# Attention's small products placed behind the maxima in each step, one product fewer for the turned shift, and maxima and later work one step on

## The reference

```python
b, n, _ = x.shape                      # 2, 1024
h, d = (HEADS, DIM_HEAD)               # 16, 64
qkv = x @ w_qkv.T
q, k, v = jnp.split(qkv, 3, axis=-1)
dots = jnp.einsum('bhid,bhjd->bhij', q, k) * SCALE
m = jax.nn.softmax(dots, axis=-1)
diag = jnp.diagonal(m, axis1=-2, axis2=-1)
mu = diag.mean(axis=-1, keepdims=True)
sd = diag.std(axis=-1, ddof=1, keepdims=True)
keep = jnp.abs((diag - mu) / sd) <= Z_THRESH
valid = keep[..., :, None] & keep[..., None, :]
masked = jnp.where(valid, dots, NEG)
attn = jax.nn.softmax(masked, axis=-1)
attn = jnp.where(row_any, attn, 0.0)
out = jnp.einsum('bhij,bhjd->bhid', attn, v)
return out @ w_out.T + b_out
```

## Time and profile before

| | |
|---|---|
| median of 3 runs | 2136.2 us |
| the profiled execution | 2125.9 us |
| its span, first to last instruction | 2124.6 us |
| PE busy | 1937.1 us, 91% |
| PEld busy | 1311.4 us, 62% |
| DVE busy | 1330.8 us, 63% |
| ACT busy | 1125.2 us, 53% |
| POOL busy | 1174.0 us, 55% |

### The profile page before, as it was taken

The page is one execution under the profiler, slowest core; times in us unless marked ns, Lnnn a source line. Parts: engine busy times, 40 slices in busy tenths (PEclk is TensorE's granted clock), DMA queues, the critical chain, the costliest instruction groups (busy, mean ns, idle before and its releaser), DMA issues. The chain is left out here.

```text
span 2124.6 us, 22033 instructions
## 1 busy us (share of the span) xinstructions
PE 1937.1 (91%) x7432; PEld 1311.4 (62%) x7432; DVE 1330.8 (63%) x2215; ACT 1125.2 (53%) x1586; POOL 1174.0 (55%) x642
## 2 busy tenths in 40 slices
PE   5997899897997984799999999999999999998588
PEld 3772333332775663577777777777777777775366
DVE  5426778887535763566666666666666666665376
ACT  4327566554434444456555555555655556553354
POOL 2440647653443553266666575666665756668454
PEclk9998799899998996899999999999999999999799
DMA  2000000000001003232222222231313131300100
GB/s 88 0 1 1 0 0 1 0 0 0 1 1 44 1 23 71 55 68 49 61 57 53 57 54 65 45 73 37 73 37 73 37 73 37 71 10 12 50 5 16
DMA packets 45921, 74.46 MB, mean 35 GB/s; under 512 B 26800, under 2 KB 28400, under 8 KB 45552
## 3 DMA queue, kind: packets, MB, share of 16 engines
q1 hardware_dynamic: 43744, 72.35, 14.7%
q10 hardware_dynamic: 2032, 0.69, 0.1%
q0 software_dynamic: 32, 0.00, 0.0%
HBM read 20.85 MB, written 1.18 MB: 10 GB/s over the span
## 5 line engine op out<-in xcount | busy, mean ns | idle before, releaser
L1988 POOL TENSOR_TENSOR at_e_lo<-at_e,at_e_hi 128x1024 fp32r<-128x1024 f32 x256 | 613.8, 2398 | 396.7 <-DVE at_e_hi L1961 395.2
L1816 ACT ACTIVATE at_e<-at_ps 128x1024 f32<-128x1024 f32 x256 | 263.0, 1027 | 315.9 <-PE at_ps L1723 315.9
L1808 ACT ACTIVATE at_ps<-at_ps,at_neg_diag 128x1024 f32<-128x1024 f32 x256 | 278.6, 1088 | 116.8 <-DVE at_neg_diag L1876 116.8
L1883 DVE TENSOR_REDUCE at_row_max<-at_ps 128x1 f32<-128x1024 f32 x256 | 311.0, 1215 | 14.9 <-PE at_ps L1702 11.8
L1876 DVE CUSTOM_DVE_ANT_0 at_junk_diag<-at_ps,ident 128x128 bf16<-128x128 f32 x256 | 74.4, 291 | 323.3 <-PE at_ps L1675 323.2
L915 POOL TENSOR_TENSOR mb_work<-mb_work,mb_c 128x1024 f32<-128x1024 f32 x64 | 151.5, 2367 | 169.5 <-DVE mb_work L891 164.7
L1961 DVE CAST at_e_hi<-at_e 128x1024 fp32r<-128x1024 f32 x256 | 220.1, 860 | 30.3 <-ACT at_e L1816 29.8
L386 POOL TENSOR_TENSOR ffn_lo<-ffn_hid,ffn_hi 128x512 fp32r<-128x512 f32 x96 | 124.4, 1298 | 179.3 <-DVE ffn_hi L313 179.3
L1673 PE MATMUL at_ps<-at_k,at_q 128*128 128x512 f32 x512 | 172.6, 419 | 16.2 <-DMA at_k<-at_qk_lo 13.9
L1702 PE MATMUL at_ps<-at_k,at_q 128*128 128x512 f32 x512 | 174.3, 422 | 10.9 <-DMA at_k<-at_mask_rows 8.5
L1742 PE MATMUL at_pv_ps<-at_e_lo,at_v_hi 128*128 128x512 f32 x512 | 161.5, 397 | 8.2 <-POOL at_e_lo L1988 8.1
(11 more groups left out here) (313 smaller groups left out, 3797.9 us busy)
## 6 DMA issues: line engine op xcount, KB each, us to landing
at_q<-at_qk_hi SPq DMA_DIRECT2D x64, 256.0 KB, 3.8
at_k<-at_qk_hi SPq DMA_DIRECT2D x32, 512.0 KB, 5.9
at_q<-at_qk_lo SPq DMA_DIRECT2D x32, 256.0 KB, 6.5
at_k<-at_qk_lo SPq DMA_DIRECT2D x32, 256.0 KB, 6.3
at_recips<-at_recip_row SPq DMA_DIRECT2D x32, 256.0 KB, 3.4
ffn_h_raw<-in_h SPq DMA_DIRECT2D x2, 1024.0 KB, 8.3
at_head_w_raw<-in_w_qkv SPq DMA_DIRECT2D x32, 64.0 KB, 4.2
x<-in_x SPq DMA_DIRECT2D x4, 256.0 KB, 4.9
```

The costliest lines, as they stand in the source:

```text
L1808: act.eng.activation(ps[:], ps[:], ACT.Exp, scale=SCALE, bias=m.small["neg_diag"][s][:, blk:blk + 1], accum_out=m.small["sums"][s][:, blk: ...
L1816: act.eng.activation(m.e[e % 2][:], slot("turned_scores", h, blk)[:], ACT.Exp, scale=SCALE).then_inc(sem["at_exp"])
L1883: dve.eng.tensor_reduce(m.small["row_max"][h % SLOTS][:, blk:blk + 1], slot("best", h, blk)[:], AX.X, ALU.max).then_inc(sem["at_best_out"])
L1988: pool.eng.tensor_tensor(m.e_lo[e % 3][:], m.e[e % 2][:], m.e_hi[e % 3][:].bitcast(F32), ALU.subtract).then_inc(sem["at_lo"])
```

## The change

The order of PE's operations within a step changes: `scores` and `best` come directly behind `turned_scores`, and mean, square, mask and shift behind them. The list of slots and DVE's order follow: DVE now rounds the exponential and takes the maximum ahead of the mean's negation, the keeps, the mask rows and the shift rows. The offsets of `best` and of all that follows it (shift, turned scores, weighing, reciprocals, spread, normalising, output) rise by one, and the loops by one step. By t mod 8: shift and the first part of the values to step 5, the second part to step 1, reciprocals to 2, spread to 3, normalising to 5, output to 7. Scores, statistics, mask and QK keep their steps.

The shift's turn is one transpose of the row maxima instead of two accumulating matmuls; the flags are added on DVE, from the turned rows that `mask_rows` kept. So DVE's `shift_rows` waits for the mask rows and is a sum of two operands, and `mask_rows` waits until the shift rows of two heads before are done.

```diff
-AT_FIRST, AT_LAST = -BLK * 2, BLK * (NH - 1) + BLK * 5
+AT_FIRST, AT_LAST = -BLK * 2, BLK * (NH - 1) + BLK * 5 + 1
...
-AT_SPLIT, AT_QK, AT_SCORES, AT_STATS, AT_MEAN, AT_SQUARE, AT_MASK, AT_BEST, AT_SHIFT = -10, -7, 0, 8, 9, 10, 11, 12, 20
-AT_TURNED, AT_PV, AT_PV_OUT, AT_RECIP, AT_SPREAD, AT_NORM, AT_OUT = 22, 23, 31, 33, 34, 36, 38
+AT_SPLIT, AT_QK, AT_SCORES, AT_STATS, AT_MEAN, AT_SQUARE, AT_MASK, AT_BEST, AT_SHIFT = -10, -7, 0, 8, 9, 10, 11, 13, 21
+AT_TURNED, AT_PV, AT_PV_OUT, AT_RECIP, AT_SPREAD, AT_NORM, AT_OUT = 23, 24, 32, 34, 35, 37, 39
...
     def turn_shift(h):
         pe.wait_ge(sem["at_best_out"], h * BLK + BLK)
         slot_free(pe, c, m, "turn_shift", h)
-        turned = slot("turn_shift", h)[0:BLK, 0:P]
-        pe.eng.matmul(turned, m.small["dropped"][h % SLOTS][:], c.ident[:], start=True, stop=False)
-        pe.eng.matmul(turned, m.small["row_max"][h % SLOTS][:], c.ident[:],
-                      start=False, stop=True).then_inc(sem["at_turn_shift"])
+        pe.eng.transpose(slot("turn_shift", h)[0:BLK, 0:P], m.small["row_max"][h % SLOTS][:],
+                         c.ident[:]).then_inc(sem["at_turn_shift"])
...
         if at := due(t, AT_TURNED, BLK):
             turned_scores(*at)
+        if at := due(t, AT_SCORES, BLK):
+            scores(*at)
+        if at := due(t, AT_BEST, BLK):
+            best(*at)
         if at := due(t, AT_MEAN):
             mean(at[0])
         if at := due(t, AT_SQUARE):
             square(at[0])
         if at := due(t, AT_MASK):
             turn_mask(at[0])
-        if at := due(t, AT_SCORES, BLK):
-            scores(*at)
         if at := due(t, AT_SHIFT):
             turn_shift(at[0])
-        if at := due(t, AT_BEST, BLK):
-            best(*at)
         if at := due(t, AT_QK):
             project(at[0])
...
         if h >= 2:
             dve.wait_ge(sem[f"mask_move{h % 2}"], 16 * (h // 2))
+            dve.wait_ge(sem["at_shift"], h - 2 + 1)
         dve.eng.tensor_copy(m.mask_rows[h % 2][:], slot("turn_mask", h)[0:BLK, 0:P]).then_inc(sem["at_mask"])
...
         dve.wait_ge(sem["at_turn_shift"], h + 1)
+        dve.wait_ge(sem["at_mask"], h + 1)
         if h >= 2:
             dve.wait_ge(sem[f"shift_move{h % 2}"], 16 * (h // 2))
-        dve.eng.tensor_copy(m.shift_rows[h % 2][:], slot("turn_shift", h)[0:BLK, 0:P]).then_inc(sem["at_shift"])
+        dve.eng.tensor_tensor(m.shift_rows[h % 2][:], slot("turn_shift", h)[0:BLK, 0:P], m.mask_rows[h % 2][:].bitcast(F32),
+                              ALU.add).then_inc(sem["at_shift"])
...
         if at := due(t, AT_STATS):
             first_stats(at[0])
+        if at := due(t, AT_TURNED, BLK):
+            e = at[0] * BLK + at[1]
+            dve.wait_ge(sem["at_exp"], e + 1)
+            if e >= 3:
+                dve.wait_ge(sem["at_pv"], e - 3 + 1)
+            dve.eng.tensor_copy(m.e_hi[e % 3][:], m.e[e % 2][:]).then_inc(sem["at_hi"])
+        if at := due(t, AT_BEST, BLK):
+            best(*at)
         if at := due(t, AT_MEAN):
             negate_mean(at[0])
```

More of the change, by code:

```diff
@@ L1426, in attention_slots @@
             order.append(("turned_scores", *at))
+        if at := due(t, AT_SCORES, BLK):
+            order.append(("scores", *at))
+        if at := due(t, AT_BEST, BLK):
+            order.append(("best", *at))
         if at := due(t, AT_MEAN):
@@ L1432, in attention_slots @@
             order.append(("turn_mask", *at))
-        if at := due(t, AT_SCORES, BLK):
-            order.append(("scores", *at))
         if at := due(t, AT_SHIFT):
             order.append(("turn_shift", *at))
-        if at := due(t, AT_BEST, BLK):
-            order.append(("best", *at))
         if at := due(t, AT_QK):
```

## The result

The changed kernel takes 2149.4 us (median of 14 runs, 2144.6 to 2161.6) beside 2135.7 for the one before (14 runs, 2125.0 to 2145.0). The ratio within rounds is **1.0096**, 95% interval 1.0077 to 1.0115: 20 us slower, 16 to 25. Forecast were +27 and 2163. The medians differ by 14 only, since runs of either kernel lie in two groups some 10 us apart (2125 to 2128 and 2135 to 2145 before, 2145 to 2149 and 2156 to 2162 after) and are divided differently; lower group against lower, and upper against upper, it is about 21.

What follows compares the result with a forecast made beforehand. PE, busy 91% of the span, was taken as the bound. 29 steady heads at +0.8 (+23), one more pipeline step (+2.4) and QK's wait in filling (+2) gave +27 on the median 2136.2: 2163 us, range 2138 to 2184.

Steps and rivals of the forecast that it cites:

- QK in step 1: In step 1, QK waits for ACT's sums of the scores and starts at 3.61 instead of 2.80: +0.81 us a head.
- Waits taken from B: In steps 1 to 3 the maxima no longer wait for the exponential: -0.18 us in step 2, -0.20 in step 3.
- Shift's turn: Step 4 loses it, -0.77 us; step 5 gains a single transpose behind the maxima, +0.33.
- The mask: In step 5 the maxima wait for the mask, queued behind the spread: +0.8 us, and 0.1 for their second half.
- Mask later still: Rival, chance 0.15: mask takes 10.8 and the spread's issue queues too; +0.6 in three of four heads, 2176 us.
- POOL's hold with the mask late: Steps 5 to 7: if the mask stalls step 5 by 0.9 us, delays from POOL's later normalising vanish.
- In a head with values: Once in four heads, mask and POOL delays both hide behind the values' wait: 0 or -0.1 us.
- Sum per head: Steps 1 to 3 +0.43 us, the rest +0.37; together 0.8, times 29 heads in the steady stretch: +23.
- Filling and one more step: One more pipeline step, at 3.0 us per filling step less 0.6, +2.4; QK's wait in three filling heads, +2.
- QK's wait at +2: During filling, QK's wait for the sums in three heads adds +2 us.
- QK doesn't wait: Rival, chance 0.08: ACT's sums of step 1 are done by 2.55, when PE reaches QK; -1.06 us a head, 2107.

Runs made afterwards that it cites:

- e1: The changed kernel with QK one step earlier (step 0) and both parts of the values one step earlier; 2096.5 us, ratio 0.9815 to the kernel before.
- e8: The changed kernel with the offsets of the kernel before, keeping the new order and the single transpose; 2152.8 us, ratio 1.0099 to the kernel before.
- e9: e1 with the old order within a step (small products ahead of scores, shift ahead of maxima); 2120.9 us, ratio 0.9949 to the kernel before.
- e7: The changed kernel with only the mask's move put ahead of the spread on SP's queue; 2137.9 us, ratio 1.0034 to the kernel before.
- e2: The changed kernel with parts and head weights ahead of the reciprocals' move on SP, and mask ahead of spread; 2138.7 us, ratio 1.0027 to the kernel before.
- e4: The changed kernel with PE's and DVE's old order within a step, keeping later offsets and single transpose; 2137.8 us, ratio 0.9998 to the kernel before.
- e3: The kernel before with only the shift's turn as one transpose and the flags added on DVE; 2130.9 us, ratio 0.9971 to the kernel before.

## Why the prediction was nearly right, step by step

The direction, the two waits and their places were right. Terms, forecast and then measured, per head:

- **QK in step 1**: +0.81, measured +0.90 (5.65 to 6.55). The row taken as the price, QK's start at 3.61, became 3.72; the sentence "nothing ahead of the sums has moved" didn't price 0.1. That it is the sums which release it, e1 and e8 show from both sides.
- **Waits taken from B**: step 2 -0.18, measured -0.17; step 3 -0.20, measured -0.35. Step 2's was right; the mask's turn behind B is cheaper, 0.15 over a plain step, than the 0.31 I carried over.
- **Shift's turn**: step 4 -0.77, measured -0.76. Step 5 +0.33, measured +0.14 where the mask is on time (3.79). The same error: a turn priced by its old place ahead of B, where its share of the wait was counted with it; the same transpose ahead of B costs 0.57 in e9 (4.22 for 3.65).
- **The mask**: forecast from the first move of parts at 3.15 of step 2 to B 14.2 after that step's T. The timeline of SP after, for the head whose first B is the one shown above:

```profile
1482.29 0.59 SPq L1588 DMA_DIRECT2D at_q<-at_qk_hi  x1
...
1488.73 0.93 SPq L1616 DMA_DIRECT2D at_recips<-at_recip_row  x1
1489.70 0.73 SPq L1599 DMA_DIRECT2D at_k<-at_mask_rows  x1
```

The first move is issued 3.07 behind T of step 2 (1479.22), and the B shown above starts at 1493.60, 14.38 behind it. Since the steps between were shorter than I had them (3.99, 3.80, 3.65), B wanted the mask at 13.3 rather than 13.4. The stop is 1.3 with the second half of B (a mean over the 21 heads without values), not 0.9: the mechanism held, the size was off, and lies nearer to the 1.5 of the rival "Mask later still" than to the forecast. Windows over the transfer, beside the earlier trace rows:

```profile
1483.00:1491.00 8.00, 8.00 (x37) 6.21 (x36) 5.92 (x14) 4.47 (x6) 5.00 (x3) 1.00 0.95 204
1491.00:1492.00 1.00, 1.00 (x6) 0.83 (x5) 0.06 (x1) 0.23 (x1) 1.00 (x1) 1.00 1.22 228
...
1492.50:1493.60 1.10, 0.14 (x1) 0.00 (x1) 0.91 (x3) 0.89 (x2) 0.00 (x0) 1.00 0.01 0
```

The engines are full from the parts to 1492 and empty from 1492.5; B starts 1.1 behind that, and 3.9 behind the mask's own issue. The Trainium skill, "DMA: Bandwidth & Descriptors", section "Queues, rings and completion order", has descriptors consumed in ring order on each DMA engine; the trace agrees, with the mask 0.20 to 0.24 behind the spread in the heads counted under e7.
- **POOL's hold with the mask late**: 0, and it is 0 (step 7 is 3.66 and 5.49). With the mask on time I priced the hold at 0.8 without an output product and 0.3 with one; e2 has 1.04 (3.66 to 4.70) and 0.42 (5.49 to 5.91).
- **In a head with values** all was to hide behind their wait. Steps 0 and 1 cost 11.66 together against 10.86, step 5 is 6.55 against an old 6.53: as forecast.
- Sum per head: +0.80, measured +0.90. Step 1 (0.09) and the mask (0.4 in three heads of four) came out 0.4 dearer, the two transposes (0.15, and 0.19 in three of four) 0.3 cheaper. That the total is so close is partly luck: errors of opposite sign.
- **Filling and one more step**: +4.4, measured -8.0 in filling and +3.8 in draining, -4.2. **This is the term that failed**, in "22 steps of filling take 66 us, 3.0 each ... one full step turns into a draining one". An equal price per step was wrong: filling is made of stops for the first transfers and of PE at the lower clock, and a step more in the pipeline doesn't lengthen it. By t=24 one block less has had its maxima, its T and its weighing; that work comes back in draining, which has a full step more (3.8). Every kernel with the later offsets fills in 61 to 66 us, every one with before's in 72.5 to 73.4; e4, which has the old order, is among the first and e8, with the new one, among the second, so it is the offsets. The windows over the filling, after and then before, and PE's waits for the mask in it:

```profile
831.40:896.80 65.40, 48.74 (x164) 34.65 (x165) 25.93 (x80) 32.86 (x55) 13.23 (x18) 0.83 0.36 76
PE at_ps L1702 <- DMA at_k<-at_mask_rows: 5.4, 2, 4.6
```
```profile
821.00:894.40 73.40, 54.24 (x178) 37.87 (x179) 28.88 (x83) 34.76 (x58) 15.97 (x20) 0.80 0.32 68
PE at_ps L1702 <- DMA at_k<-at_mask_rows: 8.5, 2, 6.2
```

So of the 8.0 PE is 5.5 less busy, with 14 matmuls fewer, and stands 2.5 less (16.7 for 19.2). The stops of the first two heads for their masks are 3.1 shorter. The first of them goes with the offsets, by which B asks for its mask a step later: 4.6 after and 4.7 in e4, 5.8 in e8 and 6.2 before. Up to the first T, where both have issued the same 153 matmuls, it is this for the kernel after:

```profile
831.40:893.80 62.40, 46.01 (x153) 32.72 (x153) 24.32 (x75) 30.74 (x52) 13.23 (x18) 0.82 0.38 80
```

The one before is the first of the earlier trace rows: 47.66 busy at a granted clock of 0.78. The same matmuls took 1.65 less at 0.82. The net -4.2 is thus 2.5 less standing and 1.7 less busy time, if the step that draining gained (3.8 for the 5.5 that filling lost) is taken as busy. What makes the clock differ no experiment took apart; it stays open. The other filling term, QK's wait at +2, is there: 2.1 us in two heads.

- **A sentence that was too strong**: "Nothing can be won there by taking waits from ACT, DVE or POOL", said of the steady stretch with PE busy 1014 of 1018 us. e1 takes 22 us out of the 28 heads against before (33.98 for 34.77 each), and of these the transpose, by e3, is 2. A busy time of 99.6% held waits all the same: a matmul behind a stop is shown longer (0.74 for 0.62 in the earlier trace rows), so the length of the steps tells more than the busy time.

Together: 28 heads +25.3, filling -8.0, draining +3.8, that is +21.1, against the +21.0 of the two ends and the 20 (16 to 25) of the ratio. The forecast's 27 is 8.6 too high by filling and draining and 2 too low by the heads. The rest of the way from 2163 to 2149, some 8 us, is how the runs fall into their two groups: the prediction took its start from 2136.2, which is in the upper group, and most runs of the kernel after are in the lower. The rival "QK doesn't wait" was rightly priced as a thing that needed another order of slots: e1 made one, and gained.

## What to carry to other kernels

Where tiles go round in a ring, moving an instruction behind another changes for every later user whose reader it waits for; write the order of slots down for each kind of step, and look up in the trace when that reader ends. Here the same reorder gained 24 us or lost 21, by the place of one other product and of the work that follows it. And when work is moved a step later, follow each queue that it shares: two issues exchanged in SP's queue were worth 14 us.

## What the runs showed of the hardware

POOL's hold on DVE reaches tiny instructions. The keeps, 128x8, in the kernel before and after (shortest, median, longest in ns):

```profile
L1906 DVE TENSOR_SCALAR at_keep<-at_dev,at_limit,at_varies x32: 290/291/1127, 848.2 to 1910.5; 128x8 f32<-128x8 f32 x32
```
```profile
L1904 DVE TENSOR_SCALAR at_keep<-at_dev,at_limit,at_varies x32: 291/1132/1134, 857.3 to 1941.3; 128x8 f32<-128x8 f32 x32
```

Moved behind the maximum they fall beside POOL's subtraction and take 1.13 us rather than 0.29. The denominators' bound, 128x8 too, has a median of 1.456 before and 0.160 after, by whether POOL runs. In every run of this case each of these two that starts while POOL works ends 0.02 to 0.04 behind POOL's instruction, and each other one takes 0.29 or 0.16 to 0.17. The maximum beside them, which reads PSUM, stays at 1.22. The Trainium skill, "Advanced Engine Details and Errata", section "Mode Summary", says that two-port instructions of VectorE and those of GpSimd block each other; the rows agree for the side of VectorE, and show that size is no protection: a held instruction of 0.2 us costs what is left of the other's 2.4.
